# GpSimd's indirect transfers in numbered pairs, each pair after the landing of the one before

## The reference

```python
# tokens: 64 patches of 28x28x3 per image, 128 images, plus a class token -> (128, 65, 128)
tokens = einsum('bpi,hi->bph', patches, W) + b
h = concat([cls, tokens], axis=1) * pos_embed
# LSTM over the 65 tokens, hidden size 128, on the normalised tokens
h = h + lstm(layernorm(h), W_ih, W_hh, b_ih, b_hh)
# mixture of 16 experts on all 8320 token rows, the two most probable of each row
y = layernorm(h)
probs = softmax(y @ router_w.T + router_b); topk_p, topk_i = top_k(probs, 2)
out = h + sum over the two: topk_p * (gelu(y @ w1[e].T + b1[e]) @ w2[e].T + b2[e])
```

## Time and profile before

| what | us |
|---|---|
| timed runs, median | 675.6 |
| profiled execution, span | 771.4 |
| TensorE busy in the span | 647.2 |
| VectorE busy | 562.3 |
| ScalarE busy | 493.0 |
| GpSimd busy | 413.1 |
| 160 transfers of results, busy | 157.0 |
| 130 transfers of rows, busy | 149.2 |

### The profile page before, as it was taken

How to read it: one execution, slowest core, us unless ns; L and a number is a source line. 1 busy time by engine, 2 the same in 40 slices (tenths; PEclk the granted TensorE clock), 3 DMA queues, 4 the chain that set the end, 5 groups by cost and what they waited for, 6 DMA issues and landing times.

```text
span 771.4 us, 24553 instructions
## 1 busy us (share of the span) xinstructions
PE 647.2 (84%) x7952; PEld 594.7 (77%) x7952; DVE 562.3 (73%) x1797; ACT 493.0 (64%) x1259; POOL 413.1 (54%) x446
## 2 busy tenths in 40 slices
PE   4999999999999999988877665878888787888870
PEld 4999999999999999888875554766666666666660
DVE  3877888888888888778886444756565756677777
ACT  4678876766667666554446343657666767777783
POOL 0243344777767666655656646545555555545552
PEclk9999999999999999999997767999999999999995
DMA  8987877888888887765522222344323234444555
GB/s 318 372 263 271 277 253 251 261 267 256 276 261 267 276 244 236 236 213 182 162 64 60 71 63 73 108 123 119 111 78 98 78 93 118 138 137 131 170 177 195
DMA packets 71895, 141.67 MB, mean 184 GB/s; under 512 B 13078, under 2 KB 55650, under 8 KB 63838
## 3 DMA queue, kind: packets, MB, share of 16 engines
q1 hardware_dynamic: 62128, 121.69, 50.1%
q0 software_dynamic: 9280, 17.21, 6.4%
q10 hardware_dynamic: 366, 1.21, 0.5%
HBM read 116.35 MB, written 25.66 MB: 184 GB/s over the span
## 4 chain that ended last, share of the span: by engine, by line
PE 25%; DVE 24%; another core or an unknown queue 13%; issue 13%; ACT 4%; POOL 3%; DMA 1%; POOLq 0%; ACTq 0%; DVEq 0%; SPq 0%
PE pair L1279 14%; DVE patches L1099 7%; PE pair L1434 3%; DVE patches L1121 2%; PE pair L1325 2%; POOL sent L1235 2%; ACT pair L680 2%; PE pair L1452 2%; PE pair L1289 1%; DVE patches L1114 1%; DVE h L1172 1%; DVE patches L1107 1%; DVE patches L1132 1%; DVE field L843 1%
## 5 line engine op out<-in xcount | busy, mean ns | idle before, releaser
L1257 POOL DMA_INDIRECT back<-patches x160 | 157.0, 981 | 150.6 <-DVE patches L1114 104.6
L680 ACT ACTIVATE pair<-pair,b1s 128x256 f32<-128x256 f32 x320 | 126.3, 448 | 110.4 <-remote 51.5
L1279 PE MATMUL pair<-field,patches 128*128 128x128 f32 (+1 forms) x1408 | 173.9, 280 | 8.9 <-DMA patches<-in_x 8.6
L1279 PEld LDWEIGHTS pair<-field,patches 128*128 128x128 f32 (+1 forms) x1408 | 164.6, 194 | 9.6 <-issue 8.6
L1235 POOL DMA_INDIRECT sent<-pay,slot_own x130 | 149.2, 1148 | 40.3 <-issue 38.2
L1434 PE MATMUL pair<-patches,ex_hi 128*128 128x256 f16 x640 | 119.4, 280 | 47.8 <-DVE patches L1099 23.8
L605 ACT ACTIVATE gate<-pair,lbias 128x128 f32<-128x128 f32 x260 | 74.4, 369 | 98.1 <-PE pair L1294 88.6
L1452 PE MATMUL pair<-ex_hi,patches 128*128 x1280 | 117.4, 225 | 8.3 <-issue 6.1
L1247 POOL TENSOR_TENSOR rstd<-veps,cst 128x2 f32<-128x2 f32 (+1 forms) x68 | 58.0, 853 | 107.2 <-DVE veps L800 106.6
L1107 DVE CAST patches<-pair 128x256 f16<-128x256 f32 x80 | 33.7, 422 | 109.6 <-remote 105.2
L1434 PEld LDWEIGHTS pair<-patches,ex_hi 128*128 x640 | 56.6, 99 | 72.8 <-issue 64.0
(11 more groups left out here) (150 smaller groups left out, 1257.7 us busy)
## 6 DMA issues: line engine op xcount, KB each, us to landing
patches<-in_x SPq DMA_DIRECT2D x62, 1152.0 KB
patches<-sent SPq DMA_DIRECT2D x80, 130.0 KB
field<-in_we SPq DMA_DIRECT2D x64, 128.0 KB
field<-back SPq DMA_DIRECT2D x10, 768.0 KB
patches<-in_b SPq DMA_DIRECT2D x80, 64.0 KB
field<-in_pos SPq DMA_DIRECT2D x65, 64.0 KB
out_tower<-h SPq DMA_DIRECT2D x10, 384.0 KB
back<-patches POOLq DMA_INDIRECT x160
```

The lines of the kernel that those rows point to most:

```text
L680: last = act.activation(up[:, cols], up[:, cols], ACT.Gelu, bias=b1s[:, bass.ds(e * FC + 2 * half + i, 1)], scale=1.0 / E_SCALE)
L1257: pool.indirect_dma_start(back, bass.IndirectOffsetOnAxis(ap=dsti[j % NO][:, k:k + 1], axis=0), yo[j % NO][:, k, :], None, bounds_check=2 ...
L1279: last = pe.matmul(bank_of, l, w_, start=(c == KS and k == 0), stop=(c == KS - 1 and k == 2))
```

## The change

All 290 indirect transfers get a number k in the order in which GpSimd issues them (issue_order). They share eight semaphores in turn (k modulo 8) in place of 36. Before a transfer with an even number, GpSimd waits until the two transfers before it have landed (pair_landed); so at most two are under way. The other waits are put in terms of the same numbers: a wait for a group of buffers becomes a wait for the last transfer of the group and the one before it (landed_to), and VectorE waits, before it reuses a result buffer, for the second transfer of the tile after the buffer's last user (result_landed). What is computed and which transfers are made stays as it was.

```diff
+LANDINGS = 8
+IN_FLIGHT = 2
...
-        sent_done = [sem(f"sent_done{i}") for i in range(NP)]
+        landed = [sem(f"landed{i}") for i in range(LANDINGS)]
...
-        y_out = [sem(f"y_out{i}") for i in range(NO)]
...
+        def issue_order():
+
+            sends, order = send_slots(), []
+            for n in range(-5, AHEAD + TILES_B + 4):
+                order += [("row", t, choice) for t, choice in sends.get(n, ())]
+                j = n - AHEAD - 3
+                if 0 <= j <= TILES_B - 1:
+                    order += [("tile", j, half) for half in range(HALVES)]
+            return {what: k for k, what in enumerate(order)}
+
+        ISSUED = issue_order()
+
+        def landing(eng, k):
+
+            eng.wait_ge(landed[k % LANDINGS], 16 * (k // LANDINGS + 1))
+
+        def pair_landed(eng, k):
+
+            if k % IN_FLIGHT == 0:
+                for i in range(max(k - IN_FLIGHT, 0), k):
+                    landing(eng, i)
+
+        def landed_to(eng, k):
+
+            for i in range(max(k - IN_FLIGHT + 1, 0), k + 1):
+                landing(eng, i)
+
...
-            for q in range(NO):
-                eng.wait_ge(y_out[q], 16 * HALVES * len(range(q, tiles, NO)))
+            landed_to(eng, ISSUED["tile", tiles - 1, HALVES - 1])
+
+        def result_landed(eng, j):
+
+            landing(eng, ISSUED["tile", j + 1, HALVES - 1])
...
-            eng.wait_ge(sent_done[t % NP], (t // NP + 1) * 32)
+
+            landed_to(eng, ISSUED["row", t, 1])
...
-                        for t in range(STARTS[EARLY_GROUPS] - NP, STARTS[EARLY_GROUPS]):
-                            rows_sent(sp, t)
+                        rows_sent(sp, STARTS[EARLY_GROUPS] - 1)
...
-                        dve.wait_ge(y_out[j % NO], j // NO * 16 * HALVES)
+                        result_landed(dve, j - NO)
...
+                    k = ISSUED["row", t, choice]
+                    pair_landed(pool, k)
                     pool.indirect_dma_start(
...
-                    ).then_inc(sent_done[t % NP], 16)
+                    ).then_inc(landed[k % LANDINGS], 16)
...
+                    for half in range(HALVES):
+                        k = ISSUED["tile", j, half]
+                        pair_landed(pool, k)
+                        pool.indirect_dma_start(back, bass.IndirectOffsetOnAxis(ap=dsti[j % NO][:, half:half + 1],
+                                                                                axis=0),
+                                                yo[j % NO][:, half, :], None, bounds_check=2 * TOKENS - 1,
+                                                oob_is_err=False).then_inc(landed[k % LANDINGS], 16)
```

More of the change, by code:

```diff
@@ L519, in step_b @@
                         sp.wait_ge(lo_done, (T - 1 - 3))
-                        for t in range(STARTS[EARLY_GROUPS] - NP, STARTS[EARLY_GROUPS]):
-                            rows_sent(sp, t)
+                        rows_sent(sp, STARTS[EARLY_GROUPS] - 1)
                     if j == EARLY:
-                        for t in range(T - NP, T):
-                            rows_sent(sp, t)
+                        rows_sent(sp, T - 1)
                         sp.wait_ge(pads, 16 * (E + 1))
@@ L1130, in step_b @@
                     if n >= NO:
-                        dve.wait_ge(y_out[n % NO], n // NO * 16 * HALVES)
+                        result_landed(dve, n - NO)
                     dve.scalar_tensor_tensor(dsti[n % NO], xt[n % 4][:, :, HID + 1], tabj[:, 0, n:n + 1],
@@ L1217, in step @@
                         if g >= 4:
-                            for k in range(STARTS[g - 4], STARTS[g - 3]):
-                                rows_sent(pool, k)
+                            rows_sent(pool, STARTS[g - 3] - 1)
                         m, a = SIZES[g], STARTS[g] % NP
                         pool.tensor_copy(slot_own[:, g % 4, :, 0:m], slotf[:, :, 0:m]).then_inc(ids_done, 1)
-                        for k in range(STARTS[g], STARTS[g + 1]):
-                            if k >= NP:
-                                rows_sent(pool, k - NP)
+                        if STARTS[g + 1] > NP:
+                            rows_sent(pool, STARTS[g + 1] - 1 - NP)
                         pool.tensor_copy(pay[:, a:a + m, HID:ROW], tag[:, STARTS[g]:STARTS[g + 1], :]
```

## The result

The changed kernel takes 980.6 us (median; 974.3 to 983.9), the kernel before 676.6 us in the same comparison: a ratio of 1.450, 95% interval 1.444 to 1.457. The direction was forecast, the size was not: 822 us, and 872 at most.

A forecast was written before the change was run, and what follows sets the result against it. TensorE was taken to bound the kernel nearly everywhere, GpSimd the changed tile stage. Tile start 427.8 + 5 + 6 + 4 = 442.8, plus 382.7, 3.6 and 12.8, gave 841.9; less 20, 822 us, range 762 to 872.

The forecast's parts named there:

- three and four sends: Token stage from slot 48: waits between a slot's sends, mostly hidden, cost 6 us for three sends, 4 us for four.
- the first profile's extra time: Whole kernel: the profiled run's extra 96 us is idle time missing from timed runs, 20 us before the first result.
- I take it as a shift that occurs once: Token stage, two sends a slot: a pair landing behind a load delays once, 5 us, bounds 0 and 102.
- rival A: Token stage: the delay repeats in every slot; 919 us fully repeated, 870 halfway; chance 0.13.
- The loop that I closed: Token stage: from a load's end over wake, pair, low half and rstd to the recurrent state, 5.5 us, fits a 6.1 us slot.
- The landing in the tile stage: Tile stage: a pair lands 1.36 us after its second transfer's end, bounds 1.14 and 1.9, giving a 4.45 us cycle.
- turns between queues by packet: Token stage: if engines alternate queues by packet, no pair stands behind a load and the 5 us would be 0.
- Both signs that the forecast is wrong: Tile-stage pair cycle under 3.9 or over 5.0 us; stage before the first tile growing by more than 35 us.
- B: Tile stage: timed runs wake and land faster than the profile shows, cycle 3.69 us, 757 us; chance 0.12.
- C: Tile stage: the granted clock falls and TensorE is the bound again for a third of tiles, 865 us; chance 0.08.
- D: Tile stage: not slower, the wait is hidden because VectorE is late anyway, 676 us; chance 0.03.
- E: Token stage: faster, since fewer transfers compete with the loads; only 0.3 us at the end to win; chance 0.02.

The follow-up runs named there:

- e10: Changed kernel, but a pair waits for the pair four before it, up to eight transfers under way; 674.5 us, ratio 1.0006.
- p0_before: The kernel before, profiled again with no edit; 676.1 us, span 674.3 us.
- e6: Kernel before plus the pair wait on token rows alone, with the load of patches cut to 2 chunks; 730.4 us, ratio 1.083.
- e9: As e6, with the loads of a position and of a weight piece also cut to 16 partitions; 714.0 us, ratio 1.060.
- e7: Kernel before plus the pair wait on tiles alone, with the bias load cut to 16 partitions; 813.5 us, ratio 1.207.
- e8: As e7, with the load of a tile's rows also cut to its last two columns; 807.9 us, ratio 1.197.
- e1: Kernel before plus one wait: a token's first send waits until both rows of the token before have landed; 772.4 us, ratio 1.145.
- e2: Kernel before plus one wait: a tile's two transfers wait for those of the tile before; 850.0 us, ratio 1.259.

## Why the prediction was wrong, step by step

| term | forecast | measured | miss |
|---|---|---|---|
| first result in before (771.4 profile, less 20) | 407.8 | 413.6 | +6 |
| slots with two sends | +5 | +42 | +37 |
| three and four sends, and up to the first result | +10 | +53 | +43 |
| first result to the last transfer's end | 385 | 454 | +69 |
| from there to the end | 14.2 | 13.2 | -1 |
| sum | 822 | 976 | +154 |

**Right.** What is queued behind the wait, and that GpSimd becomes the bound of the tile stage. The wake: 0.84 us taken, 0.85 us in the chain of the changed kernel. The gap of 0.30 us and the 0.97 us of a transfer. The numbering at zero (e10). VectorE held by its buffers, 174 us, though at line 1132 (now 1162) alone. That the first profile's extra time is missing from timed runs (p0_before). That the clock falls without TensorE becoming the bound: the line of shares above has 1% for PE.

**The step "I take it as a shift that occurs once" failed**, and rival A, with a chance of 0.13, was the mechanism: its 102 us for 30 slots were too many, its sign was right. The loop that I closed ran from a load's end over the pair, rstd and the recurrent state, 5.5 us in a slot of 6.1. GpSimd closes another: a pair, its landing behind the loads, the wake, the next pair. The rows for it stood there. The second transfer, ahead of the low half, starts at 159.36 and landed near 166.3: 6.9 us; with the 0.84 us of the wake and the 1.3 us from a pair's first transfer to its second that is 9.1 us, more than a slot, in every slot. In the changed kernel it is 7.94 us in the case shown (203.01 to 210.95) and 216.2 / 30 = 7.2 us in the mean. e6 and e9 show that the load decides: with it light, the same waits are hidden.

**Three and four sends: the same step.** I priced one wait of 1.9 us in every other slot against 1.65 us of idle time before rstd. But a slot of three sends is one and a half cycles of GpSimd. In the changed kernel pairs there start at 364.17, 369.56 and 374.70; one and a half of these cycles of 5.4 and 5.1 us are 7.9 us, and the stretch from slot 48 to the last state is 131.6 us for some 16 slots, 8.2 us each. e9 shows waits of 2.2 to 2.4 us even on a quiet queue.

**The landing in the tile stage was mis-sized.** I took 1.36 us after the second transfer's end, "nearer the quiet value since fewer transfers will be under way". The forecast's cycle of 4.45 us is right where nothing stands beside the pair. To see that, each cycle from one tile's pair to the next is set beside what the sync queue issues in it, from 0.3 us before its start to 1.5 us before its end:

| cycles of the changed kernel with | count | mean, us |
|---|---|---|
| nothing issued by the sync queue | 20 | 4.49 |
| loads of a tile's rows and of a bias | 36 | 5.19 |
| the same and a load of padding rows | 11 | 5.71 |
| a load of a chunk of `back` | 6 | 7.31 |

For in most cycles the landing that starts the next pair also starts the next tile's loads. In the 36 with rows and bias alone the second transfer lands 2.96 us after issue (median), that is 1.99 us after its end. How much of this is the bias, e7 shows: with it cut to 16 partitions, the 40 cycles with the same two loads take 4.60 us in the mean. The mean cycle was 5.22 us instead of 4.45: 87 x 0.77 = 67 us, nearly the whole 69. Some 40 us of that lie in the cycles with a tile's loads (36 x 0.74 + 11 x 1.26), 17 us in those with chunks (6 x 2.86), most of the rest where rows of tokens are sent among the tiles. Fewer transfers under way shortened nothing. My upper bound of 1.9 us was short too; it was read from the last moving packets, not from a landing.

What the Trainium skill gives for such a transfer, by the estimate in the prediction (page "DMA: Bandwidth & Descriptors", section "Anatomy of one DMA — SWDGE (gpsimd) path"), 2.15 us, agrees with 2.08 us at the quiet end of the stage and 2.2 us in e8. That estimate has no term for loads beside it: 3.1 us beside a bias load, 4.9 us beside a token's loads.

The prediction drew from turns between queues by packet that no pair would stand behind a load, and said that the rows disagree. The runs do show pairs harmed by the loads: 4.9, 3.7 and 2.6 us in e1, e6 and e9, with less and less beside them. But by the Trainium skill, page "DMA: Bandwidth & Descriptors", section "Queues, rings and completion order", an engine finishes a whole packet, typically some 9 to 17 descriptors, before it turns to the next queue. The 38 pieces of the earlier trace rows are 9.2 KB each (0.35 MB / 38), 2.4 for each of 16 engines; if each is one descriptor, this is less than one such packet, and neither these rows nor the runs speak against the turns. The order in which the engines took the pieces is not shown.

The sign that GpSimd's idle time would no longer be put down to VectorE did not come, for the reason told above. TensorE is busy 58% of the tile stage, not 70%. Both signs that the forecast is wrong came: the cycle is over 5.0 us in the mean, and the stage before the first tile grew by 95 us (413.6 to 508.8), not by 35 at most. Rivals B, C, D and E fell with the result.

## What to carry to other kernels

A wait for an engine's own last transfers costs, each time, the way from issue to landing and a wake, less what the engine does in between; compare this cycle with the engine's own share of a slot before asking what the other engines hide. The way has to be read beside the loads that will be issued at the same moment, since the wait itself lines them up. If transfers have to be limited, a window that always lets some go on costs far less than draining a group: four under way cost 3% as a window and 20% as groups, eight as a window nothing.

## What was unexpected of the hardware

The smaller load does the harm: the 64 KB of a bias, one row of 512 bytes read once for each of 128 partitions, take 3.1 us to land (e2) and add 0.8 us to the landing of a transfer beside them. The 130 KB of a tile's rows land in 2.1 us (e7), and cutting them takes off 0.1 us. The number of pieces alone is not the reason: in e8 the load of a tile's rows is 256 pieces of 8 bytes, twice as many as the bias has, and transfers beside it land in 2.2 us. No run tells whether it is the repeated row or the moment: the bias load is issued 0.4 us before the pair's second transfer (645.13 and 645.54), the load of the rows 1.2 us before it.
